# VectorE takes a unit's maxima ahead of dividing the probabilities of the unit before it, in two attentions of a two-stream kernel

## The chip, the cores and the metric

The program runs on one core of one Trainium2 chip. The metric is the device time of one execution in microseconds (us). The engines are TensorE (PE in the profile: matmuls and transposes), VectorE (DVE), ScalarE (ACT), GpSimd (POOL) and SyncE (SP, which here only issues DMAs). Each works through its own list of instructions in order and waits on semaphores for the others.

## The reference, cut to what matters

Eight samples of 256 tokens by 128 features pass through two blocks. Block 0 is an attention over selected keys (8 heads) followed by a feed-forward part that holds two layers, each with a local attention over windows of 64 tokens (8 heads of 64). Block 1 is a plain attention (16 heads) and a mixture of 16 experts. What the change touches is the softmax of the first attention and of the two local ones:

```python
# first attention: scores over the selected keys
scores = (jnp.einsum('bhld,bhlkd->bhlk', q_c, k_c) + jnp.einsum('bhld,blkd->bhlk', q_r, key_r)) * scale
attn = jax.nn.softmax(scores.astype(jnp.float32), axis=-1).astype(v.dtype)
out = jnp.einsum('bhlk,bhlkd->bhld', attn, v)
...
# local attention, twice
sim = jnp.einsum('bhwid,bhwjd->bhwij', bq, bk)
sim = jnp.where(mask, -jnp.finfo(sim.dtype).max, sim)
attn = jax.nn.softmax(sim, axis=-1)
out = jnp.einsum('bhwij,bhwjd->bhwid', attn, bv)
```

## The kernel before, in words

**Two streams.** The eight samples run as two streams of four rounds. Each stream has its own half of the chip's working memory (`arena0`, `arena1`) and its own four PSUM banks. Each engine's program is written as one generator per stream (`tensor_stream`, `scalar_stream`, `vector_stream`, `pool_stream`, `sync_stream`), cut into slots with names: `A0` to `A8` for the first attention, `W0.l` to `W5.l` for the local attention of layer `l`, and others. `TURNS` holds, for each engine, how many slots of one stream are run before it changes to the other. Nothing is decided at run time: the order of slots on each engine is fixed.

**Units.** Each of the three attentions is done in four units `u` = 0 to 3: half `T = u // 2` of the queries (128 rows) by half of the heads (4 heads). A unit of the first half has 128 keys, one of the second half 192. In the first attention each head has 32 gathered keys more. Counting four rounds, two streams and three attentions there are 24 passes of four units, 96 units in all. The steps of a unit, by line of the kernel before:

- TensorE, scores into banks 0 and 1: `att_scores` (L612) and `win_scores` (L664). Before unit u it waits for `u_bias` of unit u-1, since the banks are read until then.
- VectorE, `maxima` (L1477): adds the mask, writes the masked scores to the arena and takes the largest of each row, one instruction for each head, each followed by a small read of the accumulator. In the first attention a reduction over the gathered keys stands ahead (L1631). Then the bias of the exponential, L1634 or L1678, which signals `u_bias`.
- ScalarE, four exponentials with their row sums (L1268, L1320), after `u_bias`; they signal `u_exp`.
- VectorE, `normed`: the reciprocal of the sums (L1462), then the probabilities times it (L1465, and L1468 for the tail of units 2 and 3, L1472 for the gathered keys); it signals `u_prob`.
- TensorE, `turn_probs`: four transposes into bank 2 (L624) after `u_prob`, two more of the tail into bank 3 (L629).
- ScalarE copies bank 2 (L1114, `u_pt_act`), VectorE bank 3 (L1484, `turned_out`, units 2 and 3), TensorE multiplies with the values (`att_values` L647 and L651, `win_values` L680 and L688), and ScalarE copies the result (`u_out`).

**What a slot holds.** In slot `A{i}` or `W{i}.l` TensorE does the scores of unit i, the values of unit i-2 and the transposes of unit i-1, in this order. ScalarE copies the output of unit i-2, takes the exponentials of unit i and copies the transposes of unit i-1. VectorE, before, divides unit i-1, takes the maxima and bias of unit i, and copies the tail of unit i-1.

**Matmuls that compute nothing.** `keep_busy` (L550) issues matmuls of a constant bf16 matrix into a bank that is free. How many stand at each place is written out in `BUSY`. They stand ahead of the wait at which TensorE is expected to idle, and they run whether or not it would have to wait. In an attention slot they stand ahead of the wait for `u_prob` and ahead of the wait for the values' operands.

Of the kernel before, what the change touches and what calls it, by code (L numbers as in the profile page):

```python
# [303 lines left out]
def program(nc, A, out, idx_scratch, score_scratch):  # L304
    ctx = ExitStack()
    with ctx:
# [127 lines left out]
        def keys(T):  # L434
            return P if T == 0 else WMAX
# [1007 lines left out]
        def vector_stream(dve, st, s):  # L1443
# [88 lines left out]
            for r in range(ROUNDS):  # L1532
# [67 lines left out]
                for p in range(6):  # L1600
# [17 lines left out]
                    yield f"G{p + 1}"  # L1618
                yield "G7"
                for i in range(6):  # L1620
                    if 0 < i < 5:
                        T, half = (i - 1) // 2, (i - 1) % 2
                        normed(0, i - 1, m.probs_a[T][:, 4 * half:4 * half + 4, :], m.tail_a[half])
                    if i < 4:
# [8 lines left out]
                        maxima(i, n, probs, mask_a_bf[:, P * T:P * T + n], lambda h: mx_gathered[s][:, i, h:h + 1])  # L1633
                        dve.tensor_scalar(nb[s][:, i, :], mx[s][:, i, :], -SCALE_A, None, ALU.mult).then_inc(*one("u_bias"))  # L1634
                    if i in (3, 4):
                        turned_out(0, i - 1, m.PTa[(i - 1) % 2])
# [19 lines left out]
                for l in range(2):  # L1656
# [11 lines left out]
                    for i in range(6):  # L1668
                        if 0 < i < 5:
                            n = keys((i - 1) // 2)  # L1670
                            probs = m.probs_w[(i - 1) % 3][:, 0:4 * n].rearrange("p (h n) -> p h n", h=4)
                            normed(1 + l, i - 1, probs, m.tail_w[(i - 1) % 2])
                        if i < 4:
                            dve.wait_ge(*at("u_mm", 4 * l + i + 5))
                            n = keys(i // 2)
                            maxima(i, n, m.probs_w[i % 3][:, 0:4 * n].rearrange("p (h n) -> p h n", h=4),
                                   mask_w_bf[:, P * (i // 2):P * (i // 2) + n], lambda h: MASKED)
                            dve.scalar_tensor_tensor(nb[s][:, i, :], mx[s][:, i, :], -1.0, cqs[s][:, i // 2, 4 * (i % 2):4 * (i % 2) + 4],  # L1678
                                                     ALU.mult, ALU.mult).then_inc(*one("u_bias"))
                        if i in (3, 4):  # L1680
                            turned_out(1 + l, i - 1, m.PTw[(i - 1) % 2])
                        yield f"W{i}.{l}"
# [396 lines left out]
```

## Time and profile before

| | |
|---|---|
| median of 3 runs | 1540.59 us (1540.41 to 1545.72) |
| the profiled execution | 1545.81 us, of which 1544.0 us is the span of the profile |
| PE busy | 1352.1 us (88% of the span) |
| of this `keep_busy` | 303.4 us |
| DVE busy | 926.0 us (60%) |
| ACT busy | 862.4 us (56%) |
| POOL busy | 324.2 us (21%) |
| granted TensorE clock, mean | 0.969 of full speed |

An engine's busy time and its idle time add up to the span. A matmul's end is modelled in the profile, so a busy TensorE is not one at its peak. In the views a wait is told as idle time ahead of an instruction, with the instruction that ended it.

### The profile page before, as it was taken

The numbers are of one execution on the slowest core, as the hardware profiler recorded it, in microseconds if no ns is written. First come the engines' busy times: TensorE is split into PE (matmuls) and PEld (weight loads), VectorE is DVE, ScalarE is ACT, GpSimd is POOL, SyncE is SP. The second block draws the span as 40 slices with busy tenths as digits, with TensorE's granted clock in tenths as the row PEclk, the third lists the DMA queues.
The fourth block names the chain that finished last, engine by engine and source line by source line (L and its number), as shares of the span: only waits on it lengthen the run. The fifth ranks groups of instructions, "written<-read, shape, count | busy, mean of one in ns | idle before, by whom it ended". The sixth has DMA issues, their size and how long they took to land.

```text
span 1544.0 us, 30598 instructions
## 1 busy us (share of the span) xinstructions
PE 1352.1 (88%) x11816; PEld 966.8 (63%) x11816; DVE 926.0 (60%) x3062; ACT 862.4 (56%) x2231; POOL 324.2 (21%) x420
## 2 busy tenths in 40 slices
PE   5888989898898998988899899888899899888797
PEld 4556657576666566665676566666577567556576
DVE  4755585745565756565366576656446756866634
ACT  3344666554544657545575365754566536665483
POOL 0522030201232211200152112120015310302002
PEclk8989999899999999999999999999999999999999
DMA  8121000000102100000011110000001210000000
GB/s 273 54 61 27 7 1 1 1 4 1 49 21 62 23 5 2 1 1 5 8 42 31 55 23 2 2 1 1 5 8 42 73 24 14 1 1 1 1 1 7
DMA packets 45617, 36.45 MB, mean 24 GB/s; under 512 B 32992, under 2 KB 37536, under 8 KB 44960
## 3 DMA queue, kind: packets, MB, share of 16 engines
q1 hardware_dynamic: 45472, 34.50, 7.8%
q8 instruction: 93, 1.52, 0.4%
q14 instruction: 52, 0.43, 0.1%
HBM read 25.46 MB, written 7.44 MB: 21 GB/s over the span
## 4 chain that ended last, share of the span: by engine, by line
PE 29%; DVE 11%; ACT 7%; issue 2%; POOL 1%; SPq 0%; DMA 0%; POOLq 0%; DVEq 0%; ACTq 0%
PE ps L550 4%; PE ps L757 2%; PE ps L578 2%; ACT arena L1320 2%; PE ps L695 2%; DVE arena L1477 2%; PE ps L743 2%; PE ps L735 2%; DVE small L1726 1%; ACT arena L1114 1%; ACT arena L1268 1%; PE ps L926 1%; PE ps L680 1%; PE ps L1020 1%; PE ps L986 1%
## 5 line engine op out<-in xcount | busy, mean ns | idle before, releaser
L1114 ACT ACTIVATE arena<-ps 128x512 f32<-128x512 f32 (+7 forms) x560 | 251.9, 481 | 229.9 <-PE ps L688 33.2
L550 PE MATMUL ps<-mean_mat 128*128 128x256 bf16 x2038 | 303.4, 282 | 6.8 <-ACT arena L1114 3.4
L550 PEld LDWEIGHTS ps<-mean_mat 128*128 128x128 bf16 x2038 | 192.1, 101 | 97.7 <-issue 55.5
L1901 POOL TENSOR_TENSOR arena<-arena 128x512 f32<-128x512 f32 x64 | 81.3, 1271 | 461.5 <-DVE arena L1497 461.3
L1320 ACT ACTIVATE arena<-arena,small 128x192 f32<-128x192 f32 (+1 forms) x256 | 129.8, 509 | 33.5 <-DVE small L1678 33.0
L1726 DVE TENSOR_REDUCE small<-ps 128x4 f32<-128x1024 f32 x64 | 75.3, 1218 | 25.6 <-PE ps L986 25.3
L1615 DVE TENSOR_TENSOR gath<-ps,rank_tab 96x512 f32<-96x512 f32 x96 | 63.3, 683 | 43.9 <-PE ps L578 43.6
L1779 DVE TENSOR_TENSOR arena<-arena,ps 128x512 f32<-128x512 f32 x64 | 42.8, 686 | 73.1 <-ACT arena L1414 57.9
L1477 DVE CUSTOM_DVE_ANT_0 arena<-ps,mask_w_bf 128x192 f32<-128x192 f32 (+1 forms) x256 | 67.4, 319 | 22.5 <-PE ps L664 22.5
L1370 ACT ACTIVATE arena<-ps 128x512 f32<-128x512 f32 x128 | 66.0, 603 | 23.5 <-PE ps L1020 23.4
L757 PE MATMUL ps<-w_experts,arena 128*128 128x128 f32 x544 | 69.8, 280 | 10.2 <-DVE arena L1779 6.8
L1268 ACT ACTIVATE arena<-arena,small 128x224 f32<-128x224 f32 (+1 forms) x128 | 56.6, 443 | 38.4 <-DVE small L1634 38.3
L757 PEld LDWEIGHTS ps<-w_experts,arena 128*128 128x128 f32 x544 | 63.9, 192 | 20.0 <-issue 8.1
L1118 ACT ACTIVATE arena<-ps 128x256 f32<-128x256 f32 x48 | 18.3, 382 | 99.7 <-PE ps L553 99.7
L695 PE MATMUL ps<-w_wqkv,arena 128*128 128x512 f32 x128 | 62.8, 613 | 11.5 <-DVE arena L1497 6.2
L1405 ACT ACTIVATE arena<-ps,arena 128x128 f32<-128x128 f32 x128 | 36.6, 371 | 62.8 <-PE ps L757 56.2
L624 PE MATMUL ps<-packed,arena 128*128 128x128 f32 x384 | 60.3, 280 | 11.9 <-DVE arena L1465 5.6
L1450 DVE TENSOR_TENSOR arena<-ps,arena 128x256 f32<-128x256 f32 x48 | 20.3, 423 | 83.3 <-ACT arena L1124 83.2
L1465 DVE TENSOR_TENSOR arena<-arena,small 128x512 f32<-128x512 f32 x96 | 66.4, 692 | 3.3
L743 PE MATMUL ps<-arena,w_experts 128*128 128x256 f32 x272 | 66.2, 383 | 1.0 <-DVE arena L1516 0.8
L1180 ACT ACTIVATE arena<-ps 128x512 f32<-128x512 f32 x64 | 37.1, 595 | 53.3 <-PE ps L695 49.5
L735 PE MATMUL ps<-arena,w_experts 128*128 128x256 f32 x272 | 65.3, 380 | 0.0
(278 smaller groups left out, 2907.3 us busy)
## 6 DMA issues: line engine op xcount, KB each, us to landing
idxb<-idx_scratch SPq DMA_DIRECT2D x24, 512.0 KB, 5.1
score_scratch<-arena SPq DMA_DIRECT2D x96, 64.0 KB, 1.7
w_experts<-in_experts SPq DMA_DIRECT2D x3, 1088.0 KB, 16.5
w_wqkv<-in_wqkv SPq DMA_DIRECT2D x1, 1536.0 KB, 9.5
arena<-score_scratch SPq DMA_DIRECT2D x96, 16.0 KB, 2.1
arena<-arena SPq DMA_DIRECT2D x96, 16.0 KB, 1.8
arena<-in_x SPq DMA_DIRECT2D x8, 128.0 KB, 2.3
out_x<-arena SPq DMA_DIRECT2D x8, 128.0 KB, 1.9
```

The costliest lines, as they stand in the source:

```text
L550: mm(to, still[:, 0:P], still, start=True, stop=True)
L695: mm(bank[j], m.sh[:, cols(k)], wqkv[:, l, 512 * j:512 * j + 512], start=True, stop=True).then_inc(*one("qk_mm"))
L735: last = mm(bank[j // 2][:, L * (j % 2):L * (j % 2) + L], experts[:, 0, e, :], m.hT, start=True, stop=True)
L743: last = mm(to[:, L * (j % 2):L * (j % 2) + L], experts[:, 1, e, :], m.hT, start=True, stop=True)
L757: last = mm(bank[2 + j // 2][:, 256 * (j % 2) + P * k:256 * (j % 2) + P * k + P], m.moe_h[:, L * j + P * k:L * j + P * k + P], experts[:, ...
L1114: return act.activation(dst, src, ACT.Copy)
L1268: ins = act.activation(probs, probs, ACT.Exp, bias=nb[s][:, i, h:h + 1], scale=SCALE_A, accum_out=ls[s][:, i, h:h + 1])
L1320: ins = act.activation(probs, probs, ACT.Exp, bias=nb[s][:, i, h:h + 1], scale=cqs[s][:, T, hh_:hh_ + 1], accum_out=ls[s][:, i, h:h + 1])
L1465: ins = dve.tensor_tensor(part, part, bc(rl[s][:, u, :], 2, P), ALU.mult)
L1477: ins = dve.tensor_tensor_reduce(masked[:, h, 0:n], bank[h % 2][:, n * (h // 2):n * (h // 2) + n], mask, 1.0, least(h), ALU.add, ALU.max, ...
L1726: st.mark(dve.tensor_reduce(to, src, AX.X, ALU.max))
L1901: ins = pool.tensor_tensor(own, own, turned, ALU.add)
```

## The change

In the local attentions VectorE now does, in slot `W{i}`, the maxima and bias of unit i first and then divides unit i-1. In the first attention the same holds for slots 1 and 3. In slot 2 the division of unit 1 still stands ahead of the maxima of unit 2. In slot 4 there are no maxima, and the order is what it was. So of the 96 divisions 64 have changed places with the maxima of the next unit: 16 in the first attention, 48 in the local ones. No instruction is added or removed, the other engines' programs are word for word the same, and so are the order of slots and the number of matmuls in `keep_busy`. All lines behind move by one to five.

```diff
@@ first attention, vector_stream
+                def normed_a(u):
+                    T, half = u // 2, u % 2
+                    normed(0, u, m.probs_a[T][:, 4 * half:4 * half + 4, :], m.tail_a[half])
+
                 for i in range(6):
-                    if 0 < i < 5:
-                        T, half = (i - 1) // 2, (i - 1) % 2
-                        normed(0, i - 1, m.probs_a[T][:, 4 * half:4 * half + 4, :], m.tail_a[half])
+                    if i == 2:
+                        normed_a(1)
                     if i < 4:
                         T, half = i // 2, i % 2
                         n, probs = keys(T), m.probs_a[T][:, 4 * half:4 * half + 4, :]
...
                         dve.wait_ge(*at("u_mm", i + 1))
                         maxima(i, n, probs, mask_a_bf[:, P * T:P * T + n], lambda h: mx_gathered[s][:, i, h:h + 1])
                         dve.tensor_scalar(nb[s][:, i, :], mx[s][:, i, :], -SCALE_A, None, ALU.mult).then_inc(*one("u_bias"))
+                    if i in (1, 3, 4):
+                        normed_a(i - 1)
                     if i in (3, 4):
                         turned_out(0, i - 1, m.PTa[(i - 1) % 2])
@@ local attentions
                     for i in range(6):
-                        if 0 < i < 5:
-                            n = keys((i - 1) // 2)
-                            probs = m.probs_w[(i - 1) % 3][:, 0:4 * n].rearrange("p (h n) -> p h n", h=4)
-                            normed(1 + l, i - 1, probs, m.tail_w[(i - 1) % 2])
                         if i < 4:
                             dve.wait_ge(*at("u_mm", 4 * l + i + 5))
...
+                        if 0 < i < 5:
+                            n = keys((i - 1) // 2)
+                            probs = m.probs_w[(i - 1) % 3][:, 0:4 * n].rearrange("p (h n) -> p h n", h=4)
+                            normed(1 + l, i - 1, probs, m.tail_w[(i - 1) % 2])
                         if i in (3, 4):
                             turned_out(1 + l, i - 1, m.PTw[(i - 1) % 2])
```

The engines' programs, as built, show it at three places. A row is a line of the kernel, the operation, what it writes and reads, the shape, and the semaphores that it waits for; the last digit of a semaphore's name is the stream. ISA is the instruction that masks and takes the maximum, and the ISA row of shape 128x1 its accumulator read.

VectorE, stream 0, slot `W1` of the second local attention in round 0, before:

```order
L1462 RECIPROCAL small<-small 128x4 [waits u_exp0]
L1465 TENSOR_TENSOR arena<-arena,small 128x512 [waits dve_step]
L1477 ISA arena,small<-ps,mask_w_bf 128x128 [waits u_mm0]
L1477 ISA small 128x1
L1477 ISA arena,small<-ps,mask_w_bf 128x128
```

The division of unit 0 stands ahead of the maxima of unit 1. The same slot in the changed kernel:

```order
L1477 ISA arena,small<-ps,mask_w_bf 128x128 [waits u_mm0]
L1477 ISA small 128x1
L1477 ISA arena,small<-ps,mask_w_bf 128x128
L1477 ISA small 128x1
L1477 ISA arena,small<-ps,mask_w_bf 128x128
L1477 ISA small 128x1
L1477 ISA arena,small<-ps,mask_w_bf 128x128
L1477 ISA small 128x1
L1679 SCALAR_TENSOR_TENSOR small<-small 128x4 [waits dve_step]
L1462 RECIPROCAL small<-small 128x4 [waits u_exp0]
L1465 TENSOR_TENSOR arena<-arena,small 128x512 [waits dve_step]
```

The division now stands behind the wait for the scores of unit 1 (`u_mm0`), behind four maxima and behind the bias.

TensorE, stream 0, the same slot, alike in both kernels; `u_prob0` is what the division signals:

```order
L664 MATMUL ps<-arena 128x128 [waits u_bias0]
L664 MATMUL ps<-arena 128x128 x3
L550 MATMUL ps<-mean_mat 128x256 x8
L624 MATMUL ps<-packed,arena 128x128 [waits u_prob0]
L624 MATMUL ps<-packed,arena 128x128 x3
```

Nothing moved here: scores of unit 1, eight matmuls of `keep_busy`, then the transposes of unit 0.

VectorE, stream 0, first attention in round 0, in the changed kernel, from the bias of unit 1 on:

```order
L1637 TENSOR_SCALAR small<-small 128x4 [waits dve_step]
L1462 RECIPROCAL small<-small 128x4 [waits u_exp0]
L1465 TENSOR_TENSOR arena<-arena,small 128x4x128 [waits dve_step]
L1472 TENSOR_TENSOR arena<-arena,small 128x4x32
L1462 RECIPROCAL small<-small 128x4 [waits u_exp0]
L1465 TENSOR_TENSOR arena<-arena,small 128x4x128 [waits dve_step]
L1472 TENSOR_TENSOR arena<-arena,small 128x4x32
```

The division of unit 0 moved behind the bias of unit 1. That of unit 1 (the second reciprocal) stayed ahead of the maxima of unit 2, so the two divisions now stand one after the other.

## Rows read from the trace of the kernel before

**Rows 1.** The page, part 1: busy us, share of span, instructions.
```profile
PE 1352.1 (88%) x11816; PEld 966.8 (63%) x11816; DVE 926.0 (60%) x3062; ACT 862.4 (56%) x2231; POOL 324.2 (21%) x420
```

**Rows 2.** The page, groups of instructions: busy, mean ns of one | idle before.
```profile
L550 PE MATMUL ps<-mean_mat 128*128 128x256 bf16 x2038 | 303.4, 282 | 6.8 <-ACT arena L1114 3.4
```

**Rows 3.** Waits of PE, whole span: us in total, times, longest us.
```profile
PE ps L612 <- DVE small L1634: 9.9, 10, 4.2
PE ps L624 <- DVE arena L1465: 5.6, 5, 1.5
PE ps L664 <- DVE small L1678: 5.2, 5, 1.9
```

**Rows 4.** Timeline, 217.4 to 226.5: start us, us, engine, instruction, [idle before <- releaser].
```profile
217.81 0.71 PE L664 MATMUL ps<-arena 64*128 64x128 f32 x8 [0.33 <-DVE small L1678]
218.45 1.05 PE L550 MATMUL ps<-mean_mat 128*128 128x256 bf16 x8
...
219.84 0.18 DVE L1462 RECIPROCAL small<-small 128x4 f32<-128x4 f32 x1 [1.38 <-ACT arena L1320]
...
220.66 0.28 DVE L1477 CUSTOM_DVE_ANT_0 arena<-ps,mask_w_bf 128x128 f32<-128x128 f32 x1
...
220.79 0.66 PE L624 MATMUL ps<-packed,arena 128*128 128x128 f32 x4 [1.29 <-DVE arena L1465]
...
221.62 0.16 DVE L1678 SCALAR_TENSOR_TENSOR small<-small 128x4 f32<-128x4 f32 x1
221.82 0.49 ACT L1320 ACTIVATE arena<-arena,small 128x128 f32<-128x128 f32 x1 [2.01 <-DVE small L1678]
```

**Rows 5.** Timeline, 659.5 to 663, stream 1, second local attention, slot W2.
```profile
660.30 0.92 PE L664 MATMUL ps<-arena 64*128 64x192 f32 x8
...
660.61 0.18 DVE L1462 RECIPROCAL small<-small 128x4 f32<-128x4 f32 x1 [2.09 <-ACT arena L1320]
...
661.15 0.66 PE L680 MATMUL ps<-arena 128*64 128x128 f32 x8
661.43 0.35 DVE L1477 CUSTOM_DVE_ANT_0 arena<-ps,mask_w_bf 128x192 f32<-128x192 f32 x1
...
661.74 0.66 PE L624 MATMUL ps<-packed,arena 128*128 128x128 f32 x4
...
662.66 0.26 DVE L1678 SCALAR_TENSOR_TENSOR small<-small 128x4 f32<-128x4 f32 x1
```

**Rows 6.** Timeline, 86 to 89.6: the first of the 64 places, first attention.
```profile
86.95 0.28 DVE L1472 TENSOR_TENSOR arena<-arena,small 128x128 f32<-128x128 f32 x1
...
87.36 0.72 PE L612 MATMUL ps<-arena 64*128 64x128 f32 x8
...
88.23 0.35 DVE L1477 CUSTOM_DVE_ANT_0 arena<-ps,mask_a_bf,small 128x128 f32<-128x128 f32 x1 [0.80 <-PE ps L612]
...
88.78 0.60 PE L624 MATMUL ps<-packed,arena 128*128 128x128 f32 x4
...
89.44 0.17 DVE L1634 TENSOR_SCALAR small<-small 128x4 f32<-128x4 f32 x1
```

**Rows 7.** Timeline, 1412.8 to 1417.5: the last of the 64 places.
```profile
1413.19 0.92 PE L664 MATMUL ps<-arena 64*128 64x192 f32 x8
...
1415.52 0.17 DVE L1462 RECIPROCAL small<-small 128x4 f32<-128x4 f32 x1
...
1416.33 0.42 DVE L1468 TENSOR_TENSOR arena<-arena,small 128x256 f32<-128x256 f32 x1
...
1417.08 0.60 PE L624 MATMUL ps<-packed,arena 128*128 128x128 f32 x4
```

**Rows 8.** Windows: length, busy of PE PEld DVE ACT POOL, PEclk; the sixteen attention stretches.
```profile
82.00:109.00 27.00, 22.49 (x175) 16.38 (x175) 13.36 (x56) 14.41 (x51) 7.51 (x12) 0.81 0.27 76
652.00:672.00 20.00, 15.87 (x146) 11.63 (x145) 13.61 (x55) 12.85 (x45) 2.04 (x2) 1.00 0.00 1
...
sum 453.00, PE 390.28 PEld 287.53 DVE 297.79 ACT 311.74 POOL 71.47; mean PE 24.39 PEld 17.97 DVE 18.61 ACT 19.48 POOL 4.47
```

## The prediction, written before the changed kernel ran

> **What bounds the kernel now.** I read the page first. TensorE is busy for 1352.1 us of the span of 1544.0, VectorE for 926.0, ScalarE for 862.4 [rows 1]. TensorE runs its list in order and every unit passes through it, so the span is TensorE's busy time plus its idle time, 191.9 us. Its busy time can't fall: the change leaves its program alone, and 303.4 us of it is the matmuls of `keep_busy`, which run whether or not there is anything to wait for [rows 2]. So I ask one question: how much idle time of TensorE does the change take away, and how much does it add?
>
> Then I read who makes TensorE wait. The waits for a bias, which the change brings forward, are 9.9 us in the first attention and 5.2 us in the local ones, 15.1 us together; the largest wait for divided probabilities is 5.6 us [rows 3]. Small sums: `keep_busy` already fills most of the time in which TensorE would wait.
>
> The timelines show what hides behind this. In rows 4 (stream 0 nearly alone) VectorE sits idle 1.38 us until the exponentials are done, divides, takes the maxima, and only then can ScalarE go on, after 2.01 us of idleness [rows 4]. VectorE and ScalarE take turns. This is what the change unties.
>
> **The change, step by step.** *What moves.* 64 divisions go behind the maxima and bias of the next unit. No instruction is added. Those maxima read the scores that TensorE computes in the same slot in which it transposes the probabilities of the unit before. So from now on there is, in each of the 64 slots, a chain that starts and ends on TensorE: scores end, VectorE sees it, four maxima, bias, reciprocal, division, TensorE sees it, transposes begin. Before, the division didn't need the scores.
>
> *The length of this chain.* For units of 128 keys in the local attention maxima and bias take 220.66 to 221.78, 1.12 us, and the division lasts from 219.84 to about 220.74, 0.90 us; TensorE follows 0.05 later [rows 4]. I take 0.05 us for VectorE to start behind the scores, the same as that. Sum 2.12 us. With 192 keys maxima and bias take 661.43 to 662.92, 1.49 us, there with a bias of 0.26 where 0.16 is usual [rows 4, 5]: 1.4, chain 2.4 us. Where unit 2 is divided the tail is added, 1415.52 to 1416.75, 1.23 us [rows 7]: chain 2.75 us. In the first attention maxima and bias take 88.23 to 89.61, 1.38 us; the start behind the scores 0.15; and the division has one instruction of 0.28 us more, some 1.1 us in all [rows 6]: chain 2.6 to 2.7 us. For its slot 3 I estimate 3.2 us from these (1.38 + 0.28 for wider maxima, 1.1 + 0.33 for the tail, 0.1 to both sides).
>
> *What TensorE has to do meanwhile.* From the end of the scores to the start of the transposes I took the distance in each of the 64 slots from the timeline. Four examples:
> - rows 4: 218.52 to 220.79, 2.27 us. The chain fits. The bias would come at about 219.7 instead of 221.78 and ScalarE's wait of 2.01 us would go. This slot is better off.
> - rows 5: 661.22 to 661.74, 0.52 us against 2.4. TensorE would wait 1.9 us.
> - rows 6 (the first of the 64): 88.08 to 88.78, 0.70 us against 2.7. It would wait 2.0 us.
> - rows 7 (the last): 1414.11 to 1417.08, 2.97 us against 2.75. That fits, but VectorE comes free only at 1415.52, and from there maxima and division reach to 1418.2: 1.1 us late.
>
> Over all, the distance averages 0.63 us in slot 1 of the first attention (8 places) and 2.6 in its slot 3 (8); 1.41, 1.73 and 1.58 us in slots 1, 2 and 3 of the local attentions (16 each). For each place I took the longer of the chain and of TensorE's own work between the two (so a wait that is there today isn't counted twice), less the distance of today: 15.9, 7.1, 11.8, 11.9 and 18.8 us. Sum **+65.4 us**, 1.0 us for a place; 58 of the 64 fall short, the rest gain a little. The reason is that the scores often end only after the division is over: `keep_busy` and the other stream stand ahead of them on TensorE, so VectorE had the division done before it got them.
>
> *What it takes away.* TensorE's 15.1 us of waiting for a bias [rows 3] lie, place by place: 4.6 behind unit 0, whose bias has no division ahead of it in either kernel; 5.9 ahead of slot 3 of the first attention, where the division of unit 1 still precedes the maxima of unit 2; and 4.8 where the bias now comes sooner. So -4.8 us, at best -15.1.
>
> *What is late next, and what absorbs.* The stalls delay both streams, since TensorE's queue holds both. But while TensorE stands, the other stream's work on ScalarE and VectorE goes on, and its waits may shrink. In the sixteen stretches with attention TensorE idles 453.0 - 390.3 = 62.7 us [rows 8]; 14.9 us of it lie inside the 64 distances and are already counted, 15.1 are the waits for a bias, and about 33 are other waits. Most of these hang on something that TensorE issued shortly before, and move along with it. I take a third, -11 us; the bounds are 0 and -33.
>
> ScalarE gets its bias sooner, so the exponentials end sooner, but the division stands behind the maxima, which wait for TensorE: this gain ends there. The DMAs of the divided gathered keys wait for `u_prob` of units 1 and 3; those divisions keep their places and shift with the rest. POOL has no work in these slots that waits for a division.
>
> **Sum:** +65.4 - 4.8 - 11 = about +50 us. The profiled execution took 1545.81 us, so it would take 1596. It stands 5.2 us over the median of the runs, so for the median I say 1540.6 + 50 = **1591 us**, +3.2%.
>
> **A rule against the trace.** The view of waits shows TensorE idle for 15.1 us on this bias [rows 3], and the place in rows 4 is better off. The Trainium skill, page "Perfetto Trace Analysis", section "Optimization Strategy", says to take the busiest engine's gaps, find what blocks it there, and make that start sooner, which is just what this change does. By that rule alone one would forecast the first rival below. The distances in rows 5 and 6 say that here the cure lengthens another path into the same engine.
>
> **The rivals.**
> - *Bias waits go, nothing comes.* The chain costs nothing wherever TensorE's own work between scores and transposes lasts at least 2.1 to 3.2 us. If the filling matmuls and the values' matmuls covered it (they do in 6 of the 64 places), all waits for a bias would go: 1540.6 - 15.1 = 1525 us. For: rows 4. Against: rows 5 and 6, and an average distance of 1.6 us. 6%.
> - *It cancels.* Of the stalls all that can be absorbed is, and the places like rows 4 set the pace of the passes in which a stream is nearly alone: its alternation of 4.0 us a unit (217.81 to 221.82 [rows 4]) is shortened by up to the 2.01 us of that place. At an assumed 20 of the 64 places that is 20 to 40 us, against 17 to 50 us of stalls: 1535 to 1550. 8%.
> - *Half the stalls are absorbed.* +65.4 - 15.1 - 33 = +17 is the lowest; between it and the forecast lies about +28: 1569 us. 20%.
> - *VectorE comes late and TensorE's clock falls.* Counting from when VectorE is free in each place, as in rows 7, gives +72 instead of +65.4 at 11 places. And more idleness may lower the clock: the stretch 82 to 109, with TensorE busy 22.49 of 27 us, had a granted clock of 0.81, while 652 to 672, busy 15.87 of 20, kept 1.00 [rows 8]. Idleness alone doesn't decide, but if all 453 us lost 0.08 of the clock more, somewhat under half of what the first of these stretches has lost, with TensorE busy 86% of the time, that is 31 us: 1591 + 7 + 15 to 31 = 1613 to 1629. 16%.
> - *The change doesn't do what it says* holds in one part: slot 2 of the first attention keeps its order. That is in the sum; it has no chance of its own.
>
> The Trainium skill, page "TensorE: Matmul & The Clock Gate", section "HAM oscillation — how this bites in real kernels", says that idle gaps between bursts of matmuls send TensorE back to its half clock. Taken alone it would put most of the chance on the fourth rival; the stretch at 652 us speaks against that.
>
> **How the numbers follow.** The forecast has 50%, the rivals 6, 8, 20 and 16. The range is 1560 to 1625 us: from just above the lowest sum (+17) to about the clock's upper end. A measurement of this kernel tells 0.5%, 7.7 us, from no change. Faster by more: the first rival and a little of the second, 0.07. Within: 0.07. Slower: 0.86.
>
> **What would show it.** In the profile of the changed kernel TensorE's busy time stays at 1352 us (more only if the clock falls) and the idle time grows to about 242. The waits of the transposes (L624) for a division, of which the largest entry is 5.6 us now [rows 3], come to 50 us or more in all. The waits for a bias fall to about 10 us. VectorE's waits ahead of the reciprocal, 1.38 and 2.09 us in the two places shown [rows 4, 5], are mostly gone, and it waits ahead of the maxima instead. The forecast is wrong if TensorE's idle time ahead of the transposes grows by less than 30 us, or if it grows as said and the idle time elsewhere falls by as much.

## The result and the profile after

The changed kernel takes 1610.37 us (median, 1609.37 to 1613.71), the kernel before, run beside it, 1540.5 us. The ratio is 1.0439 (95% interval 1.0418 to 1.0460): slower by 69.9 us. The forecast was 1591 us with a range of 1560 to 1625. The direction and the mechanism came out, the size not fully.

The profiled execution took 1610.83 us with a span of 1609.0, 65.0 us more than the span before. The page after, part 1, as [rows 1] (busy us, share of span, instructions), and the row of part 2 with the granted clock in tenths of full speed over 40 slices:

```profile
PE 1374.4 (85%) x11816; PEld 977.7 (61%) x11816; DVE 927.7 (58%) x3062; ACT 866.7 (54%) x2231; POOL 321.2 (20%) x420
...
PEclk9889999999999899999998989999999899999999
```

TensorE's busy time grew by 22.3 us. Its idle time is 1609.0 - 1374.4 = 234.6 us, 42.7 more than the 191.9 before. The other engines do the same work in about the same time (within 5 us). So 42.7 of the 65.0 us are recorded as waiting, and 22.3 as the same 11816 matmuls being busy for longer.

The waits of PE after, as [rows 3] (us in total, times, longest us):

```profile
PE ps L624 <- DVE arena L1472: 32.4, 16, 2.8
PE ps L624 <- DVE arena L1465: 30.1, 28, 2.1
PE ps L624 <- DVE arena L1468: 20.6, 18, 2.2
...
PE ps L664 <- ACT arena L1114: 4.1, 7, 1.0
...
PE ps L664 <- DVE small L1679: 4.1, 4, 1.9
...
PE ps L612 <- DVE small L1637: 0.6, 2, 0.5
```

The transposes (L624) now wait 83.1 us for the three instructions of the division, where the largest such entry was 5.6 us. The waits for a bias fell from 15.1 us [rows 3] to 4.7.

Who has stopped waiting, and who has begun, stands in the groups of instructions by shape, of after (busy, mean ns of one | idle just before them, and what ended it):

```profile
L624 PE MATMUL ps<-packed,arena 128*128 128x128 f32 x384 | 66.0, 298 | 83.4 <-DVE arena L1472 32.4 <-DVE arena L1465 30.1 <-DVE arena L1468 20.6
L612 PE MATMUL ps<-arena 64*128 64x192 f32 x128 | 19.6, 440 | 0.2 <-DVE small L1637 0.2
L680 PE MATMUL ps<-arena 128*64 128x128 f32 x512 | 43.0, 290 | 2.0 <-DVE arena L1484 1.7
L647 PE MATMUL ps<-arena 128*32 128x128 f32 x256 | 14.1, 293 | 1.3 <-DVE arena L1484 1.1
```

and the same groups of before:

```profile
L624 PE MATMUL ps<-packed,arena 128*128 128x128 f32 x384 | 60.3, 280 | 11.9 <-DVE arena L1465 5.6 <-DVE arena L1472 4.4 <-DVE arena L1468 1.6
L612 PE MATMUL ps<-arena 64*128 64x192 f32 x128 | 16.7, 386 | 9.4 <-DVE small L1634 9.4
L680 PE MATMUL ps<-arena 128*64 128x128 f32 x512 | 42.1, 285 | 9.4 <-ACT arena L1114 7.1 <-DVE arena L1484 1.7
L647 PE MATMUL ps<-arena 128*32 128x128 f32 x256 | 14.1, 293 | 8.3 <-ACT arena L1114 7.1 <-DVE arena L1484 1.1
```

The idle time ahead of the transposes rose by 71.5 us. Ahead of the values' matmuls (L680, L647) it fell from 17.7 to 3.3: the copy of the transposed probabilities (L1114), for which they waited 14.2 us, is no longer what they wait for in any place. TensorE has stood still at the transposes on the way, so the copy has time to end before TensorE gets there. With the waits for a bias (-10.4) and -4.0 for all the rest the balance is +71.5 - 10.4 - 14.4 - 4.0 = +42.7.

**The place of rows 5.** Timeline of after, the same slot (stream 1, second local attention, `W2`):

```profile
685.79 0.92 PE L664 MATMUL ps<-arena 64*128 64x192 f32 x8
...
686.64 0.66 PE L680 MATMUL ps<-arena 128*64 128x128 f32 x8
686.75 0.36 DVE L1477 CUSTOM_DVE_ANT_0 arena<-ps,mask_w_bf 128x192 f32<-128x192 f32 x1 [3.78 <-PE ps L664]
...
687.99 0.16 DVE L1679 SCALAR_TENSOR_TENSOR small<-small 128x4 f32<-128x4 f32 x1
688.07 0.17 DVE L1462 RECIPROCAL small<-small 128x4 f32<-128x4 f32 x1
...
688.27 0.69 DVE L1465 TENSOR_TENSOR arena<-arena,small 128x512 f32<-128x512 f32 x1
...
689.11 0.63 PE L624 MATMUL ps<-packed,arena 128*128 128x128 f32 x4 [1.82 <-DVE arena L1465]
```

VectorE has been idle for 3.78 us. In [rows 5] it divides ahead of the maxima at this place. Here the division stands behind the maxima, and these wait for the scores. From the end of the scores (686.71) the chain runs through maxima, bias, reciprocal and division to the transposes at 689.11: 2.40 us. TensorE waits 1.82 of it.

**The place of rows 4** went as said too, and does not help:

```profile
226.29 0.71 PE L664 MATMUL ps<-arena 64*128 64x128 f32 x8 [0.33 <-DVE small L1679]
...
226.94 1.05 PE L550 MATMUL ps<-mean_mat 128*128 128x256 bf16 x8
...
227.05 0.29 DVE L1477 CUSTOM_DVE_ANT_0 arena<-ps,mask_w_bf 128x128 f32<-128x128 f32 x1
...
228.22 0.49 ACT L1320 ACTIVATE arena<-arena,small 128x128 f32<-128x128 f32 x1
...
229.28 0.66 PE L624 MATMUL ps<-packed,arena 128*128 128x128 f32 x4 [1.30 <-DVE arena L1465]
```

ScalarE starts its exponentials 1.93 us after the scores began (228.22 - 226.29), where it was 4.01 us before [rows 4], and its wait of 2.01 us for the bias is gone. Yet the transposes start 2.99 us after the start of the scores, where it was 2.98: in this slot nothing is gained on TensorE, which waits 1.30 us as it did.

**One stretch of work in both kernels.** From the scores of unit 0 in stream 1's first attention of round 1 to the end of stream 0's transposes of unit 3 in the first local attention, both streams in attention. Window of before, then of after (length, then busy us of PE, PEld, DVE, ACT, POOL, then the granted clock):

```profile
521.30:548.10 26.80, 23.83 (x239) 17.12 (x238) 20.88 (x103) 22.16 (x80) 2.33 (x2) 1.00 0.10 20
```

```profile
534.40:569.40 35.00, 27.94 (x239) 19.11 (x238) 21.05 (x103) 22.60 (x80) 2.33 (x2) 0.85 0.08 15
```

The same 239 matmuls take 35.0 us for 26.8. TensorE's idle time in it went from 2.97 to 7.06 us, its busy time from 23.83 to 27.94, and the granted clock from 1.00 to 0.85: part of the stretch ran at 1.2 GHz, where all of it had run at 2.4.

### The profile page after: what moved, and what is told of

Its sections match the earlier page's. It is cut to its first block, busy times and chain, and to the rows that moved or that the text cites. A ratio compares the mean times of both kernels' runs of the same rounds, so it can differ in the third digit from the quotient of the medians.

```text
span 1609.0 us, 30598 instructions
## 1 busy us (share of the span) xinstructions
PE 1374.4 (85%) x11816; PEld 977.7 (61%) x11816; DVE 927.7 (58%) x3062; ACT 866.7 (54%) x2231; POOL 321.2 (20%) x420
## 4 chain that ended last, share of the span: by engine, by line
PE 32%; DVE 12%; ACT 3%; issue 2%; POOL 1%; SPq 0%; DMA 0%; POOLq 0%; DVEq 0%; ACTq 0%
PE ps L550 4%; DVE arena L1477 3%; PE ps L578 2%; PE ps L757 2%; PE ps L624 2%; PE ps L695 2%; PE ps L743 2%; PE ps L735 2%; PE ps L664 1%; DVE small L1731 1%; PE ps L926 1%; DVE arena L1465 1%; PE ps L986 1%; PE ps L612 1%; PE ps L1020 1%
## 5 line engine op out<-in xcount | busy, mean ns | idle before, releaser
L1114 ACT ACTIVATE arena<-ps 128x512 f32<-128x512 f32 (+7 forms) x560 | 255.6, 483 | 299.5 <-PE ps L688 51.4
L550 PE MATMUL ps<-mean_mat 128*128 128x256 bf16 x2038 | 308.6, 286 | 6.5 <-ACT arena L1114 3.3
L550 PEld LDWEIGHTS ps<-mean_mat 128*128 128x128 bf16 x2038 | 194.2, 102 | 101.5 <-issue 58.3
L624 PE MATMUL ps<-packed,arena 128*128 128x128 f32 x384 | 66.0, 298 | 83.4 <-DVE arena L1472 32.4
L1477 DVE CUSTOM_DVE_ANT_0 arena<-ps,mask_w_bf 128x192 f32<-128x192 f32 (+1 forms) x256 | 67.6, 320 | 92.7 <-PE ps L664 92.4
L624 PEld LDWEIGHTS ps<-packed,arena 128*128 128x128 f32 x384 | 44.0, 148 | 102.9 <-DVE arena L1472 34.4
L1370 ACT ACTIVATE arena<-ps 128x512 f32<-128x512 f32 x128 | 66.1, 604 | 22.2 <-PE ps L1020 22.0
L1477 DVE CUSTOM_DVE_ANT_0 arena<-ps,mask_a_bf,small 128x192 f32<-128x192 f32 (+1 forms) x128 | 41.5, 381 | 45.9 <-PE ps L612 45.3
L743 PE MATMUL ps<-arena,w_experts 128*128 128x256 f32 x272 | 66.2, 383 | 1.0 <-DVE arena L1516 0.8
```

What stands on the lines that cost most here:

```text
L550: mm(to, still[:, 0:P], still, start=True, stop=True)
L624: last = pe.transpose(bank[2][:, cols(h)], probs[:, h, :], ident[:, :])
L743: last = mm(to[:, L * (j % 2):L * (j % 2) + L], experts[:, 1, e, :], m.hT, start=True, stop=True)
L1114: return act.activation(dst, src, ACT.Copy)
L1370: act.activation(m.PT1[v][:, q, :, :].rearrange("p j n -> p (j n)"), bank[q], ACT.Exp, scale=SCALE_1)\
L1477: ins = dve.tensor_tensor_reduce(masked[:, h, 0:n], bank[h % 2][:, n * (h // 2):n * (h // 2) + n], mask, 1.0, least(h), ALU.add, ALU.max, ...
```

## The experiments

They ask four questions: where in the attentions the time goes; whether it is the wait for the scores or the maxima behind it; whether the waiting itself or the clock costs; and whether the kernel before was bound as the prediction said. Each kernel was run beside the kernel before on the same chip, and the ratios and differences from it stand against those runs (1544 to 1545 us), not against the 1540.5 us above. Differences between two changed kernels can therefore be off by a few us.

### Each attention alone

The change in the local attentions alone, and in the first attention alone. The order is set by a predicate that stands ahead of and behind the maxima; this is its core:

```diff
+                        if 0 < i < 5 and not division_last(s, r, 1 + l, i):
+                            normed_w(l, i - 1)
                         if i < 4:
                             dve.wait_ge(*at("u_mm", 4 * l + i + 5))
...
+                        if 0 < i < 5 and division_last(s, r, 1 + l, i):
+                            normed_w(l, i - 1)
# local_only: g > 0 and i < 4     first_only: g == 0 and i in (1, 3)
```

> Only the divisions of the two local attentions go behind the maxima (48 of the 64 places); the first attention is as before. Stall theory (TensorE waits in each slot for scores, maxima, bias, division): in the changed kernel 48.6 of the 81.1 us that TensorE waits ahead of the transposes of these 64 places are in the local attentions, so 60% of the +69.9 us, about +42: 1582 us (1575 to 1590). Rival (VectorE's order delays the other stream, mostly where both streams are in attention at once): the local attention in the slots shared with the first attention is hit as soon as either of the two is changed, so most of the loss would come already here: 1595 us or more.

> Only the 16 divisions of the first attention go behind the maxima; the local ones are as before. Stall theory: 32.5 of 81.1 us of waits, so about +28: 1568 us (1560 to 1575), and together with the kernel that changes the local attentions alone +70. Rival (the other stream is delayed): the two alone would add up to clearly more than +70.

Measured: the local attentions alone 1587.18 us (1.0271, 1.0239 to 1.0302), the first alone 1565.05 (1.0146, 1.0115 to 1.0177): +42 and +20 us. That is 0.9 us for each of 48 places and 1.3 for each of 16. Both lie in their ranges, and together they are +62, where the rival had clearly more than +70. The other 8 us come only when both are there, or lie within what the two intervals leave open (5 us each). Both parts cost, and nearly in proportion to the stalls that the distances gave (42.5 and 23.0 us net).

### The wait for the scores alone

The order of before, but VectorE waits for the scores of unit i ahead of dividing unit i-1, in the same 64 places. The maxima stay behind the division.

```diff
                 for i in range(6):
+                    if i in (1, 3):
+                        dve.wait_ge(*at("u_mm", i + 1))
...
                     for i in range(6):
+                        if 0 < i < 4:
+                            dve.wait_ge(*at("u_mm", 4 * l + i + 5))
```

> The kernel before, order untouched (division, then maxima and bias), but VectorE waits for the scores of unit i before it divides unit i-1, at the same 64 places as the change. So of the chain scores, maxima, bias, division, transposes only the maxima and bias are taken out (1.1 to 1.65 us). From the distances of the kernel before: TensorE's stalls ahead of the transposes 24 us where the changed kernel has 81, net +9 us; the bias comes up to 0.9 us later at 43 places, which adds up to as much again in the waits of the scores for it: 1552 to 1568 us. If it were the wait for scores alone that costs (the early scores took away only 20 of 44 us), it comes to 1580 us or more; if it were the maxima in front alone, to 1545 or less.

Measured 1562.33 us (1.0114, 1.0093 to 1.0135), +18. The timeline of this kernel at the place of [rows 5]:

```profile
670.63 0.92 PE L669 MATMUL ps<-arena 64*128 64x192 f32 x8
...
671.60 0.18 DVE L1467 RECIPROCAL small<-small 128x4 f32<-128x4 f32 x1 [2.75 <-PE ps L669]
671.81 0.69 DVE L1470 TENSOR_TENSOR arena<-arena,small 128x512 f32<-128x512 f32 x1
```

The reciprocal waited 2.75 us for the scores (L669 here) although the exponentials were ready. TensorE's idle time ahead of the transposes is 23.6 us in all, as forecast (24), against 11.9 before and 83.4 with the change. The number was hit, but one of its terms was not: the later bias was to cost TensorE as much again, and its waits for a bias stayed at 14.8 us (15.1 before). So the wait for the scores alone gives about 18 of the 70 us, and the other 52 come only with the maxima and the bias between it and the division. A chain of about 1 us mostly fits into the distances of 0.6 to 2.6 us, one of 2.1 to 3.2 doesn't.

### The scores of units 2 and 3 a slot earlier

If the dependency on the scores is the cause, scores that TensorE has computed at the end of the slot before must take it away in slots 2 and 3 (40 of the 64 places). The order of after, and:

```diff
                 for i in range(6):
-                    if i < 4:
+                    if i < 2:
...
                         turn_probs(0, u, m.probs_a[u // 2][:, 4 * (u % 2):4 * (u % 2) + 4, 0:P], m.tail_a[u % 2])
+                    if i in (1, 2):
+                        att_scores(i + 1)
# the same with win_scores in the local attentions
```

> The changed kernel, with TensorE's scores of units 2 and 3 moved from the start of slots 2 and 3 to the end of slots 1 and 2, behind the transposes. The maxima then find their scores ready, and the chain from the scores to the transposes no longer starts and ends in the same slot. Stall theory: the waits ahead of the transposes in slots 2 and 3 go (14.4 us in the first attention, 29.7 in the local ones), those of slot 1 (37.0) stay: 1610 - 40, about 1570 us (1558 to 1580). Rival (what costs is VectorE's order, which is the same here): 1600 us or more.

Since moving the scores is an edit of its own, it was also run with the order of before on VectorE (early_before), and with the division ahead in slot 1 and behind in slots 2 and 3 (early_keep1).

> The kernel before, with TensorE's scores of units 2 and 3 moved to the end of slots 1 and 2, and VectorE's order untouched (division, then maxima and bias). Stall theory: now TensorE waits at the end of the slot for the bias, which stands behind the division and the maxima, 1.1 to 1.6 us after the probabilities, of which the transposes cover 0.6: 0.5 to 1.0 us in 48 places, +24 to +48: 1565 to 1588 us, waits of the scores for a bias of 30 us or more. Rival (earlier scores help by themselves, in any order of VectorE): 1540 us or less.

> As the kernel with early scores (scores of units 2 and 3 at the end of slots 1 and 2), but in slot 1 of all attentions the division stays ahead of the maxima as before, and in slot 2 of the first attention it does so in all kernels. So the division is behind the maxima in 40 places, and in none of them do the maxima wait for scores of the same slot. Stall theory: hardly a stall is left, and the waits for a bias are gone as well: 1525 to 1545 us, with luck below the kernel before. Rival (VectorE's order costs by itself): 40 of 64 places of the loss, 1575 us or more.

| kernel | division behind in | us | ratio | idle ahead of transposes |
|---|---|---|---|---|
| early_before | none | 1556.66 | 1.0084 (1.0055 to 1.0113) | 15.4 |
| early_keep1 | slots 2 and 3 | 1564.93 | 1.0146 (1.0124 to 1.0168) | 31.8 |
| early_scores | slots 1, 2 and 3 | 1588.16 | 1.0286 (1.0259 to 1.0313) | 63.6 |

All three lie between the two expectations; early_scores missed the number of the stall theory by 18 us, early_keep1 the end of its range by 20. The steps between the rows tell more than the rows. Early scores alone cost 12 us, where the one theory had 20 or more and the other no cost at all: TensorE now comes to the scores before their bank is free. Its waits for a bias in early_before (PE's waits, whole span):

```profile
PE ps L612 <- DVE small L1638: 13.9, 15, 3.5
PE ps L664 <- DVE small L1682: 12.4, 20, 1.9
```

26.3 us against 15.1 [rows 3]. On top of that, the division behind in the 40 places whose scores were early costs 8 us, 0.2 a place; in the 24 places of slot 1, whose scores weren't, it costs 23 us, 1.0 a place. So where the scores are early most of the price in time is gone, and where they aren't it stays. That speaks for the theory. But the stalls themselves did not go, though the expectation said that they would: in the 40 places they fell from 44.1 to 24.3 us. What stays there has another cause. This is one of them, in the timeline of early_scores (the scores of this unit end at 554.42):

```profile
553.50 0.92 PE L664 MATMUL ps<-arena 64*128 64x192 f32 x8
...
553.77 0.29 DVE L1476 TENSOR_TENSOR arena<-arena,small 128x128 f32<-128x128 f32 x1
...
556.01 0.42 DVE L1488 COPY arena<-ps 128x256 f32<-128x256 f32 x1 [1.95 <-PE ps L629]
...
556.35 0.35 DVE L1481 CUSTOM_DVE_ANT_0 arena<-ps,mask_w_bf 128x192 f32<-128x192 f32 x1
...
558.94 0.65 PE L624 MATMUL ps<-packed,arena 128*128 128x128 f32 x4 [1.51 <-DVE arena L1472]
```

The scores are ready, but VectorE stands in the other stream's slot and waits 1.95 us for that stream's transposes of the tail (L629), to copy them (L1488). Only then do the maxima run, and the division behind them; before the change the division alone would have stood there. In 23 of the 40 places VectorE goes to the maxima without idling in front of them, late by 58.3 us in all, and for 35.2 of these it was idle in the other stream's slot (25.5 for L629, 9.7 for that stream's scores). 17.4 of the 24.3 us of stalls in the 40 places lie in these 23. So VectorE can also come late by a wait in the other stream. Such waits are longer where TensorE stalls more: in the changed kernel VectorE waits 76.2 us for L629, 52.7 before (waits of DVE, after and then before):

```profile
DVE arena L1477 <- PE ps L664: 92.4, 49, 5.9
...
DVE arena L1484 <- PE ps L629: 76.2, 48, 5.2
...
DVE arena L1477 <- PE ps L612: 45.3, 25, 4.9
```

```profile
DVE arena L1484 <- PE ps L629: 52.7, 40, 3.4
DVE small L1462 <- ACT arena L1320: 39.0, 25, 2.6
DVE small L1462 <- ACT arena L1268: 27.0, 20, 2.0
```

These two fences also show the exchange that the change makes: VectorE no longer waits 66 us for the exponentials (L1462; 3.5 us are left), it waits 137.7 us for the scores (L1477), where it had waited 33.4.

### What the waiting costs, and what the clock

The order of after, with 675 more matmuls of `keep_busy` ahead of the wait for `u_prob` at 58 places, as many as the stall there had room for:

```diff
                 keep_busy(bank[2][:, 0:L])
+                for _ in range(MORE.get((s, of.r, g, u), 0)):
+                    mm(bank[2][:, 0:L], still[:, 0:P], still, start=True, stop=True)
                 pe.wait_ge(*at("u_prob", 4 * g + u + 1))
```

> The changed kernel with 675 more matmuls of keep_busy at 58 of its places, ahead of the wait for the divided probabilities, as many as fit into the wait that its trace shows there (one for each full 0.115 us). They compute nothing. If the lower granted clock (0.961 against 0.969, and 22.3 us more busy time of TensorE) is a consequence of the stalls, the clock comes back to 0.967 or more and the time falls by 10 to 22 us: 1588 to 1600. If the clock has another cause, the time stays at 1610 (1605 to 1615), as the matmuls only take the place of waiting. If the waits were not there in other executions, it rises.

The opposite: the 291 matmuls of `keep_busy` that already stand between the scores and the transposes at the 64 places are left out.

```diff
-                keep_busy(bank[2][:, 0:L])
+                if u == 3 or (g, u) == (0, 1):
+                    keep_busy(bank[2][:, 0:L])
+                else:
+                    left_out[0] += int(next(busy), 36)
```

> The changed kernel without the 291 matmuls of keep_busy that stand between the scores and the transposes at the 64 places (some 0.115 us each, 33 us of TensorE's work; they compute nothing). Stall theory: scores, maxima, bias, division is a floor that TensorE's work in between does not move, so the waits ahead of the transposes grow from 83 to about 115 us and the time stays, but for the clock: 1605 to 1630 us. Rival (these slots are bound by TensorE's own work, the waits are a by-product): 33 us less, 1577 to 1585.

Measured: filled 1586.39 us (1.0271, 1.0241 to 1.0301), 24 us less than the changed kernel and 2 below the expected range. The added matmuls are busy for 84.0 us; TensorE's busy time as a whole rose by 46.0 (1374.4 to 1420.4). Thin 1638.23 us (1.0604, 1.0580 to 1.0628), 28 us more, with less to do. By the ratios the two differences are 26 and 25 us. The same stretch of work as above, in filled and then in after_thin:

```profile
531.40:563.90 32.50, 30.24 (x294) 22.25 (x293) 21.05 (x102) 22.48 (x80) 2.30 (x2) 1.00 0.09 17
```

```profile
546.20:582.30 36.10, 24.74 (x219) 17.31 (x217) 21.09 (x103) 22.88 (x80) 2.35 (x2) 0.86 0.07 15
```

With the gaps filled the clock is 1.00 again and the stretch takes 32.5 us instead of 35.0. It doesn't come back to 26.8: there is no gap left to speak of (2.3 us idle), and 5.7 us of the 8.2 stay. I read these as the chain itself, which holds TensorE whether it waits or fills (some of it may be filler that lasts longer than the wait did; the run can't tell). The other 2.5 are the clock.

For the whole span the mean granted clock c gives the time at half speed as 2 (1 - c) times the span, and half of that is work that the engine could have done (an upper bound of the loss, since it also counts half-speed time in which TensorE waits):

| kernel | span us | mean clock | at half speed | half of it |
|---|---|---|---|---|
| before | 1544.0 | 0.969 | 96 | 48 |
| after | 1609.0 | 0.961 | 126 | 63 |
| filled | 1584.5 | 0.976 | 76 | 38 |
| after_thin | 1639.9 | 0.932 | 223 | 112 |

Filled against after: 25 us less in the last column, and 24 us of time. The table is of the profiled executions; over all four executions of each the clock is 0.958 to 0.963 in after and 0.976 to 0.980 in filled. Thin against after: 49 us more in the last column, 28 us of time. Thin was expected at 1605 to 1630 and took 1638; its waits are those forecast (121.7 us ahead of the transposes, 115 expected), the excess I read as the clock, whose cost I had put too low.

### Was the kernel before bound by what TensorE has to do?

The prediction adds to TensorE's busy and idle time. Two kernels change these in the kernel before. before_thin leaves out the same 291 matmuls as after_thin; before_filled adds 236 at 39 places where TensorE waits, ahead of the transposes and ahead of the values' operands, with the edit of filled.

> The kernel before without the same 291 matmuls. Here the divisions are mostly over when TensorE reaches the transposes: by its trace the transposes could start 23 us earlier in all. Stall theory: 1518 to 1535 us if the clock holds, and up to 20 us more if it falls with the idleness (half-speed time above 97 us): 1518 to 1550. Rival (the kernel before is as little bound by TensorE's own work at these places as the changed one): 1540 or more at an unchanged clock.

> The kernel before with 236 more matmuls of keep_busy, at 39 places of the three attentions where its trace shows TensorE waiting for divided probabilities or for the values' operands, as many as fit (one for each full 0.115 us). They compute nothing. If filled waits give a higher granted clock and the clock gives the time back, as in the changed kernel (half-speed time 126 to 77 us, time -24 us), the half-speed time of 97 us falls to 75 to 90 and the time by 4 to 10 us: 1531 to 1537 us. If the clock gained there only because the stalls were many, no difference: 1538 to 1544. If the matmuls come late in executions where the wait is shorter, up to 1550.

Measured: before_thin 1548.87 us (1.0030, 1.0017 to 1.0042), before_filled 1541.59 (0.9979, 0.9966 to 0.9992). Part 1 of the page of before_thin, then its largest waits for the division (waits of PE):

```profile
PE 1323.8 (86%) x11477; PEld 943.2 (61%) x11477; DVE 927.1 (60%) x3062; ACT 862.0 (56%) x2231; POOL 323.8 (21%) x420
```

```profile
PE ps L628 <- DVE arena L1469: 15.3, 11, 2.5
...
PE ps L628 <- DVE arena L1476: 11.5, 9, 2.2
```

In the profiled execution (1544.85 us, mean clock 0.969 as in the one of before) TensorE has 28.3 us less to do and isn't done earlier: its idle time is 1543.1 - 1323.8 = 219.3, 27.4 more, of which 17.8 stand ahead of the transposes. Nearly all that was taken away came back as waiting. And before_filled, with TensorE busy for 20.6 us more, is 3 us faster. So in these slots TensorE's own work doesn't set the pace in the kernel before either. I read the loop through ScalarE and VectorE as what does (exponentials, division, transposes, copy), with `keep_busy` filling what is over; no run isolates that loop.

The median of before_thin lies in the upper part of the stall theory's range (1518 to 1550), and that part was for a fallen clock; it lies in the rival's as well, which was for an unchanged one. Over all executions the clock did fall: its mean is 0.965 in the ten of before_thin (0.961 to 0.969) and 0.972 in the thirteen of before beside them, which is some 20 us more at half speed, 10 us at most of time. The profiled execution is one of the two with the highest clock. There the 23 us of gain that the stall theory had at a clock that holds did not come. before_filled was expected at 1531 to 1537 and lies in the range for no difference (1538 to 1544), but its interval lies below 1: it is the fastest kernel here and beats the kernel before by 0.2%, with a mean clock of 0.976 over its twelve executions for 0.972.

## Why the prediction was right, and where it wasn't

**The chain, right.** Its length at [rows 5] was put at 2.4 us and measures 2.40; the wait at 1.9, and is 1.82. At the first place [rows 6] 2.0 was said and 1.73 came, at the last [rows 7] 1.1 and 1.19. The distances from scores to transposes grew by 71.1 us in all, where 65.4 was said. 58 of the 64 places were to fall short, and 58 wait for more than 0.1 us. With the 14.9 us that lay inside the distances already, the stalls were 80.3 us; the transposes of the 64 places wait 81.1.

**The waits for a bias, too small.** The sum had -4.8 (at best -15.1); it was -10.4. The step that failed is the one that kept 5.9 us ahead of slot 3 of the first attention, since the division of unit 1 still precedes the maxima of unit 2. It does, but TensorE, held up at the transposes in front, comes so late that the bias is there: idle ahead of L612 with 192 keys went from 9.4 to 0.2 us.

**The other waits, about right.** -11 was taken, with 0 and -33 as bounds. Outside the stalls of the 64 places TensorE idled 191.9 + 49.6 - 80.3 = 161.2 us by the forecast, and 234.6 - 81.1 = 153.5 in fact. 5.6 of these 7.7 us are the bias, so the absorption was 2 us larger than taken. Most of it lay in one place, the values' waits for L1114.

**The clock, the mis-sized term.** It stood at 0 in the sum and at 15 to 31 us in the fourth rival. TensorE's busy time rose by 22.3 us. Both kernels issue the same 11816 matmuls in the same order, so they can be compared one by one. Those at half clock in one of the kernels, or in both, add 15.6 us. Those at full clock in both add 6.8, and most of this is not slower work. A record of a transpose lasts 0.27 us, and the next begins 0.11 us later, so in a row each adds 0.11 us to busy time; the first behind a wait overlaps nothing and adds 0.33. 43 groups of transposes at full clock now stand behind a wait and did not before, and the first ones of all groups add 8.2 us. The matmuls of groups that wait less than before give 3.7 back, and 2.3 lie in 24 small matmuls (L1078); why these are longer was not tried. So the term that stood at 0 measured 15.6 us.

I had held the stretch at 652 us [rows 8], busy 15.87 of 20 us at clock 1.00, against a fall. It keeps 1.00 in the changed kernel too, where nearly the same work lies in this window:

```profile
678.00:701.00 23.00, 16.55 (x149) 12.01 (x149) 13.43 (x55) 13.25 (x45) 2.04 (x2) 1.00 0.00 1
```

The change touches this stretch: three of the 64 places lie in it, [rows 5] among them, and it takes 22.7 us for the work of 20. So the reading of the row was right, and the step from it to the other stretches was not. The stretch at 521 us, which had been busy 24 of 27 us, fell to 0.85. That at 214 to 250 us, with six places, kept 1.00 (223.0 to 263.3 in the changed kernel) and got 4.3 us longer. Over the sixteen stretches of [rows 8] the time at half speed rose from 44 to 85 us. What tells one stretch from another is open.

The Trainium skill, page "TensorE: Matmul & The Clock Gate", section "A second HAM failure mode: psum-queue depth-cycling", tells of a kernel in which the engine idles briefly but often between groups of matmuls and the clock swings between its two levels. The trace agrees for the kernel as a whole: here no wait ahead of the transposes is longer than 2.8 us, and the mean clock fell from 0.969 to 0.961. It does not agree in every stretch, as the one at 652 us shows.

**Sum.** Forecast +49.6 idle and 0 busy; measured +42.7 and +22.3, of which 15.6 are the clock. The errors of -7 and +22 partly cancel, and +65.0 in the profile became +69.9 between the medians, since the profiled execution of before stands above its median.

**The rivals.** *Bias waits go, nothing comes*: the first half is true, the second false. *It cancels*: at the place of [rows 4] ScalarE gains 2 us and TensorE nothing; ScalarE's waits for a bias fell only from 71.3 to 54.2 us. *Half the stalls are absorbed*: it put the lowest sum at 48.1 us taken off (15.1 and 33) and half-way at 37; 28.8 us fell elsewhere, of them 10.4 waits for a bias. *The clock falls*: in part, at its lower end; VectorE came late by more than 0.3 us in 9 places only, so its 7 us on top did not show by themselves.

**What the right answer hides.** The sum took the change in TensorE's idle time as the change in time. That came out here, as a stall that VectorE's chain causes holds up both streams. It isn't a rule: before_thin shows 27 us more idle time for 5 us, and filled 70 us less for 24. As I read it, the stalls mattered because the chain behind them was the pace, not because TensorE stood.

A rule of the Trainium skill was weighed before the run: page "Perfetto Trace Analysis", section "Optimization Strategy", find what blocks the engine and make it start sooner. No run here contradicts the sentence itself; the bias did come sooner and its waits went, by 10.4 us. What it left out, the idle time ahead of the transposes, came to seven times as much (71.5 us): what had to stand behind it on the same engine.

## What to carry to other kernels

Before a step is moved ahead of another on an engine that runs in order, write down what the step moved waits for: the one left behind now waits for that as well, and for the step's own length. If both its release and its consumer sit on the same engine and in the same slot, as scores and transposes do here, measure the distance between them on that engine; it has to be longer than the whole chain (2.1 to 3.2 us here against 0.6 to 2.6). Don't put the clock's term at nothing because one stretch with waits in it kept its clock: look at several that the change touches, and at several executions. And don't take an engine's busy plus idle time for proof that it sets the pace: take some of its filling work away and see whether the time moves.

## What the runs showed of the hardware that I had not expected

- Short waits can lower TensorE's clock. With waits of at most 2.8 us at 58 places the time at half speed rose from 96 to 126 us; with these filled by matmuls that compute nothing it fell to 76; with the filler thinned out it rose to 223 us. It isn't so everywhere: three such waits (1.46, 1.82 and 1.20 us) lie in the stretch at 678 us, which kept 1.00. In the kernel before the same thinning lowered the mean clock from 0.972 to 0.965 over all executions, though the two profiled ones have 0.969 both. In that profile the stretch at 521 us fell from 1.00 to 0.88 (before_thin):

```profile
519.50:547.00 27.50, 24.46 (x218) 16.94 (x217) 20.96 (x103) 22.23 (x80) 2.34 (x2) 0.88 0.10 19
```

- Matmuls that compute nothing can shorten a kernel: 675 more of them, busy for 84.0 us, took 24 us off the changed kernel. What else they do than hold the clock up no run shows. In the kernel before, 236 more (TensorE busy for 20.6 us more) brought 3 us.
- At full clock four transposes that follow `keep_busy` without a wait are recorded as 0.60 us (median, 62 places of before), and behind a wait as 0.66. The wait isn't the only thing that goes with it: at 15 places of before they follow a matmul of scores or values without a wait, and are 0.66 as well. In both cases only the first of the four is longer, 0.33 us for 0.27. Why was not tried.
